# A gated state-space layer and a squared-ReLU FFN on one core: the order of all engines inside a batch, the FFN square, and TensorE's loop

## The reference

```python
def attn(x, A, B_w, B_b, C_w, C_b, D_w, D_b, s_w1, s_b1, s_w2, s_b2, g_w, g_b):
    s = sigmoid(silu(x @ s_w1.T + s_b1) @ s_w2.T + s_b2)
    u = (x @ B_w.T + B_b) * s
    # h_t = h_(t-1) @ A.T + u_t, over the 1024 tokens of a batch; hs holds all h_t
    y = hs @ C_w.T + C_b + x @ D_w.T + D_b
    return y * sigmoid(x @ g_w.T + g_b)

def ffn(x):                       # plus routed experts, weighted with trunc(softmax)
    return square(relu(x @ Ws1)) @ Ws2

x = x + layernorm(attn(layernorm(x)))
x = x + layernorm(ffn(layernorm(x)))
```

## Time and profile before

| | us |
|---|---|
| median of 3 runs | 936.57 (935.44 to 937.42) |
| profiled execution | 932.95 |
| its span, first to last instruction | 931.2 |
| TensorE busy | 857.2 (92%), 4120 matmuls |
| VectorE busy | 571.1 (61%) |
| GpSimd busy | 435.1 (47%) |
| ScalarE busy | 306.7 (33%) |
| DMA | 72.91 MB, mean 78 GB/s |

### The profile page before, as it was taken

One profiled execution on the slowest core, in us unless ns is written; L12 is line 12 of the kernel. 1 busy time (PEld: TensorE's weight loads), 2 busy tenths in 40 slices (PEclk: granted clock), 3 DMA queues, 4 the chain that ended last, 5 costly groups with the idle time before them and its releaser, 6 DMA issues. The chain is left out here.

```text
span 931.2 us, 13126 instructions
## 1 busy us (share of the span) xinstructions
PE 857.2 (92%) x4120; PEld 700.5 (75%) x4120; DVE 571.1 (61%) x1344; ACT 306.7 (33%) x530; POOL 435.1 (47%) x537
## 2 busy tenths in 40 slices
PE   5589999999999999999999999999999999999974
PEld 3477877878777777877778787777777777787763
DVE  4826676477655775467753776557754677624653
ACT  3341333224332333323332233323333233422333
POOL 1342456264453545444462644535554444625455
PEclk9889999999999999999999999999999999999998
DMA  8221023122130222211222221302222120122112
GB/s 282 80 81 56 15 77 114 69 91 92 45 120 18 90 90 90 92 53 47 80 113 69 90 90 41 121 20 90 90 90 92 49 77 9 67 69 91 46 45 91
DMA packets 17289, 72.91 MB, mean 78 GB/s; under 512 B 2643, under 2 KB 5075, under 8 KB 11094
## 3 DMA queue, kind: packets, MB, share of 16 engines
q1 hardware_dynamic: 17238, 72.38, 22.0%
HBM read 38.82 MB, written 33.55 MB: 78 GB/s over the span
## 5 line engine op out<-in xcount | busy, mean ns | idle before, releaser
L1404 POOL TENSOR_TENSOR rsv<-rsv,negh 128x1 f32<-128x1 f32 x64 | 35.7, 559 | 159.1 <-DVE rsv L1083 159.1
L421 PE MATMUL TM<-gw_hi,xT_hi 128*128 128x512 f32 x256 | 107.7, 421 | 0.7 <-ACT apt L770 0.7
L421 PE MATMUL TM<-dw_hi,xT_hi 128*128 128x512 f32 x256 | 102.7, 401 | 0.8 <-ACT work L781 0.8
L423 PE MATMUL TM<-gw_hi,xT_lo 128*128 128x512 f32 x256 | 100.8, 394 | 0.0
L423 PE MATMUL TM<-dw_hi,xT_lo 128*128 128x512 f32 x256 | 100.5, 393 | 0.0
L422 PE MATMUL TM<-gw_lo,xT_hi 128*128 128x512 f32 x256 | 100.1, 391 | 0.0
L422 PE MATMUL TM<-dw_lo,xT_hi 128*128 128x512 f32 x256 | 99.7, 389 | 0.0
L842 ACT ACTIVATE work<-TM,nmz,rsz 128x512 f32<-128x512 f32 x62 | 48.2, 778 | 148.3 <-POOL nmz L1414 148.3
L1440 POOL TENSOR_TENSOR xres<-work,xres 128x512 f32<-128x512 f32 x64 | 83.7, 1308 | 6.0 <-DVE work L1087 5.9
L1079 DVE TENSOR_TENSOR work<-TM,work 128x512 f32<-128x512 f32 x64 | 44.0, 688 | 67.1 <-PE TM L423 67.1
L1444 POOL TENSOR_TENSOR work<-work,xres 128x512 f32<-128x512 f32 x62 | 81.8, 1324 | 6.3 <-ACT work L842 6.3
(11 more groups left out here) (145 smaller groups left out, 2110.5 us busy)
## 6 DMA issues: line engine op xcount, KB each, us to landing
xin<-in_x SPq DMA_DIRECT2D x16, 1024.0 KB, 6.2
xres<-in_x SPq DMA_DIRECT2D x16, 1024.0 KB, 5.5
x_scratch<-xres SPq DMA_DIRECT2D x16, 1024.0 KB, 4.8
out<-work SPq DMA_DIRECT2D x30, 512.0 KB, 2.7
xres<-in_g_w_t SPq DMA_DIRECT2D x1, 1024.0 KB, 6.8
xres<-in_D_w_t SPq DMA_DIRECT2D x1, 1024.0 KB, 7.6
work<-in_Ws SPq DMA_DIRECT2D x2, 512.0 KB, 8.8
out<-work SPq DMA_DIRECT2D x4, 256.0 KB, 2.0
```

The lines of the kernel that those rows point to most:

```text
L421: eng.matmul(ps, lhs[0], rhs[0], start=first, stop=False)
L423: return eng.matmul(ps, lhs[1], rhs[0], start=False, stop=last)
L1404: return eng.tensor_tensor(dst, src, negh[:, 0:n], ALU.pow)
```

## The change

It has five parts.

1. The order in which each engine's queue takes the helpers inside a batch is another one, for batches 0 to 6. `tail_and_scan` becomes `first_tail` (batch 0, as before), `tail` and `last_tail`; `body` is new, `last_body` is the old order without the `prep` parts. The orders of batch 7 are the old ones.
2. The FFN square: ScalarE's Square writes h2_hi directly instead of hf. VectorE's h2 multiplies max(bank, 0) with hf (the Relu) into a part of w_first and subtracts h2_hi from it, giving h2_lo. GpSimd's h2_low is gone, as is VectorE's copy.
3. The FM bank of W1f is free when VectorE has made its square (sq_ok), not after the Relu (relu_ok).
4. TensorE's loop over batches 1 to 6 is written out by Python's `range`; the other engines keep theirs.
5. Four waits of TensorE for a high part are left out, where the wait for the low part of the same tile follows.

The diff, cut to its core:

```diff
-        FM_FREED = {"w": "relu_ok", "h": "h1_ok", "b": "u_ok", "s": "s_ok"}
+        FM_FREED = {"w": "sq_ok", "h": "h1_ok", "b": "u_ok", "s": "s_ok"}
...
+        def h2_free(eng, i, rep, m):
+
+            if m:
+                eng.wait_ge(S["w2_done"], body_at("w2_done", i, m * MS - 1))
+            elif rep > 0:
+                eng.wait_ge(S["w2_done"], body_at("w2_done", i - 1, L - 1))
...
-                eng.wait_ge(S["hs_hi_ok"], body_at("hs_hi_ok", b, j))
                 eng.wait_ge(S["hs_lo_ok"], body_at("hs_lo_ok", b, j))
...
-                G(*a, 0, {2: 0})
-                W1f(*a, 1, 0, {0: 1, 2: 2})
-                W1f(*a, 1, 1, {0: 3, 2: 4})
-                G(*a, 1, {0: 5, 2: 6})
-                G(*a, 2, {0: 7, 2: 8})
-                W2(*a, 4)
-                scan_step(*a, 9)
-                W2(*a, 5)
-                scan_step(*a, 10)
-                G(*a, 3, {1: 11})
-                W2(*a, 6)
-                W2(*a, 7)
+                G(*a, 0)
+                scan_step(*a, 0)
+                W1f(*a, 1, 0, {0: 1, 2: 2})
+                scan_step(*a, 3)
+                W1f(*a, 1, 1, {2: 4})
+                scan_step(*a, 5)
+                G(*a, 1, {1: 6, 2: 7})
+                G(*a, 2, {1: 8})
+                scan_step(*a, 9)
+                W2(*a, 4)
+                W2(*a, 5)
+                G(*a, 3, {1: 10})
+                W2(*a, 6)
+                W2(*a, 7)
+                scan_step(*a, 11)
...
-            with eng.Fori(1, NB - 1) as b:
-                tail_and_scan(b, 1)
+            for b in range(1, NB - 1):
+                tail(b, 1)
                 body(b, 1)
...
                 eng.wait_ge(S["relu_ok"], body_at("relu_ok", i, KF * m + f))
-                eng.activation(hf_row(name), hf_row(name), ACT.Square).then_inc(S["sq_ok"], 1)
+                h2_free(eng, i, rep, m)
+                eng.activation(h2_hi[:, f, :], hf_row(name), ACT.Square).then_inc(S["h2hi_ok"], 1)
...
+                eng.wait_ge(S["relu_ok"], body_at("relu_ok", i, KF * m + f))
+                h2_free(eng, i, rep, m)
+                square = w_first[:, D:2 * D]
...
+                eng.scalar_tensor_tensor(out=square, in0=fm_bank(name)[:, :], scalar=0.0, in1=hf_row(name),
+                                         op0=ALU.max, op1=ALU.mult).then_inc(S["sq_ok"], 1)
                 eng.wait_ge(S["sq_ok"], body_at("sq_ok", i, KF * m + f))
-                eng.tensor_copy(h2_hi[:, f, :], hf_row(name)).then_inc(S["h2hi_ok"], 1)
+                eng.wait_ge(S["h2hi_ok"], body_at("h2hi_ok", i, KF * m + f))
+                eng.tensor_tensor(h2_lo[:, f, :], square, h2_hi[:, f, :].bitcast(F32), ALU.subtract)\
+                   .then_inc(S["h2lo_ok"], 1)
```

More of the change, by code:

```diff
@@ L1214, in body @@
             def body(b, rep):
                 a = (b, rep)
-                prep = rep + 1 < NB
+                attn(*a, 0)
+                attn_norm(*a, 0)
+                attn(*a, 1)
+                attn_norm(*a, 1)
+                hs_low(*a, 2)
+                x1_stats(*a, 0)
+                x1_stats(*a, 1)
+                ft_low(*a, 0)
+                attn(*a, 2)
+                attn_norm(*a, 2)
+                ft_low(*a, 1)
+                hs_low(*a, 3)
+                t_low(*a, 0)
@@ new lines, in body @@
+                attn(*a, 3)
+                x1_stats(*a, 2)
+                ln1_norm(b + 1, 4)
+                hs_low(*a, 4)
+                t_low(*a, 1)
+                ft_low(*a, 2)
+                ln1_norm(b + 1, 5)
+                hs_low(*a, 5)
+                attn_norm(*a, 3)
+                attn(*a, 4)
+                ft_low(*a, 3)
+                x1_stats(*a, 3)
+                hs_low(*a, 6)
+                attn(*a, 5)
+                hs_low(*a, 7)
+                attn_norm(*a, 4)
@@ new lines, in body @@
+                h1(*a, 0, 0)
+                h1(*a, 0, 1)
+                t_low(*a, 2)
+                t_low(*a, 3)
+                x1_stats(*a, 4)
+                attn_norm(*a, 5)
+                u_of(*a, 0)
+                ln1_norm(b + 1, 6)
+                x1_stats(*a, 5)
+                ln1_norm(b + 1, 7)
+                attn(*a, 6)
+                ft_low(*a, 4)
+                ft_low(*a, 5)
+                attn_norm(*a, 6)
+                h2(*a, 0, 0)
+                h2(*a, 0, 1)
```

630 lines of the change are left out of this document (361 added, 269 removed).

## The result

The changed kernel took 909.5 us (median of 4 runs, 908.57 to 910.27) against 936.67 (935.44 to 937.42), a ratio of 0.973 [0.971, 0.975]: faster by 27.2 us, where 35.6 were forecast. Its profiled execution took 909.91.

The account below looks back on a forecast made before the run. TensorE's own work and its few waits were taken to bound each loop batch; 5.7 us a batch, 34 over six, plus 0.1 (batch 0) and 1.5 (last batch) make 35.6, giving 901 us; own range 897 to 907, with rivals to 912.

Parts of the forecast that it names:

- The five waits: TensorE's waits at W2(7), T(0), FT(5), T(4), SG(1) in each loop batch all go: 5.4 us a batch.
- The residual waits: New small TensorE waits at scan steps 1, 7, 9 and T(5), charged 0.1 each: 0.4 us lost a loop batch.
- Neighbours: Isolated fp32 groups on TensorE fall from 26 to 20 a loop batch, 0.08 each: 0.5 us gained.
- TensorE's loop written out: TensorE's jump back at each loop batch's head goes: 0.16 us gained a batch.
- The square: FFN square with VectorE subtracting: zero in the loop (to +0.5), earlier W2(0) and W2(4) in the last batch, 1.5 together.
- Batch 0: FT(0) first waits for ln1_norm(0), Y(0) 3.4 us later; offset by waits and groups saved: net 0.1 gained.
- The sum: Six loop batches 34 us, first batch 0.1, last batch 1.5: 35.6 us gained in all.
- A: VectorE becomes late at scan steps 7, 9 and T(5), 1.6 us a batch more than charged: 10, 911 us; chance 0.15.
- B: A GpSimd chain is late at SG(1), the old 1.07 us wait stays: 6 us, 907; chance 0.08.
- C: TensorE's straight-line code must be fetched, 57 more instruction pieces at 2.0 us exposed: slower, 1015 us; chance 0.04.

Follow-up runs that it names:

- The splitting run: Four FT transposes drawn apart on TensorE, against the changed kernel with VectorE's loop written out, batch 0's FT(0) later and hs_low(3) earlier: 905.21 us.

## Why the prediction was right, and where its sizes were off

The time of 909.5 us lies 8.5 above the forecast's 901, outside its own range of 897 to 907 and inside the one that reaches over the rivals to 912. Two of its signs failed: a loop batch took 104.45 us, not 103.1 +- 0.7, and TensorE's waits in it were up to 0.65, not under 0.2. The others came: the wait of 3.78 before FT(0), L1455's group gone, VectorE busy for 33.3 us more, and the wait at W2(7) of the last batch (1.24).

*The five waits* were right, one by one, and with them the sign and nearly the size of a loop batch: 103.1 forecast, 104.45 measured, and 103.03 once the two residues were taken away. The forecast had seen what bounds the loop (TensorE alone) and what the order could give.

*The residual waits* were the step that failed. The part on the waits charged 0.1 each at four places (scan steps 1, 7 and 9, and T(5)), 0.4 us a batch; 1.4 came (104.45 - 103.03), at one of the four, scan step 1, and at Y(3), which it did not name. Scan step 1 was too cheap because the sum priced TensorE's jump from a row and VectorE's not at all: in the order of before that jump stands in an idle stretch of VectorE, and its first addition, though counted, made nobody wait. The Trainium skill, Runtime: NRT & Kernel Launch, Instruction fetch mechanics, says that a taken branch to code outside a small window stalls. The forecast looked for that on TensorE, where the changed order shows no cost at all; behind VectorE's jump the traces show 0.63 (2.52 - 1.89) that the run with its loop written out takes away. By that rule the trace agrees on VectorE, and so does the count of q14's pieces, 23 for 38. Y(3) was the other: "everything else has 0.6 or more" holds for hs_low(3) only at the 0.29 of the earlier trace rows, though the earlier trace rows show a VectorE operation of 0.54 stretched to 1.52 beside GpSimd. The forecast used that row only as an upper bound for the square.

*Neighbours* was mis-sized: 0.5 us a batch was forecast from the 0.08 behind each isolated group. The rows had the answer: a group of eight is followed by the next matmul after 0.79 and two groups of four after 0.35 each, and 2 x (0.35 + 0.08) is 0.86, 0.79 + 0.08 is 0.87. What merging saves behind a group it loses inside. The splitting run prices it at 0.01 to 0.05 for a group. Of the 5.8 us between 108.84 and 103.03, the gap at TensorE's jump has 0.16 and the six groups about 0.1; the five waits with their restarts have the rest, 5.5, where 5.4 were counted.

*TensorE's loop written out*: 0.8 us were forecast over the batches, and the kernel without it takes 0.8 more in its trace (1.3 timed), but by luck. The gap at TensorE's jump is gone with the loop kept as well, together with the wait ahead of it, and the 0.8 lies in VectorE's jumps. No run shows that this part of the change is worth more than nothing.

*The square*: right in the loop (nothing). In the last batch the 0.69 taken for the subtraction was 1.64 and 1.68 for the two that fall beside GpSimd's x1 and 0.69 to 0.75 for the two that do not; the forecast had 1.52 as its upper end. VectorE's square itself took 0.69, not 0.75. But the run with the square moved shows that even the right duration would not have brought the 0.5 us at W2(0): the chain over x1(7) bounds that batch. The mistake was to count a wait's end as the batch's end without asking what ends next. W2(4) waits 2.3 for 3.1 and starts 0.8 earlier, near the 1.0 forecast; TensorE comes to it 98.7 us behind G(0), for 98.6 before. Of the 1.5 forecast 0.8 came, then. The spans hide it: behind W2(4) the profiled execution of before ran at the full clock and that of after at half of it, -0.8 in sum. Where the second execution of the changed kernel kept the full clock, the last batch takes 116.1, 0.8 less than before.

*Batch 0*: the wait of 3.8 us was right to 0.1. What failed is the clock behind it, a term that the sum did not have: TensorE at half its clock (the spacing is 0.43 for 0.23, the lower of its two levels, 1.2 GHz) for 3 us, some 1.4 us lost. Together 0.1 gained was forecast, and 1.5 were lost (3.0 in the second trace, where it lasted 6 us). The trace of before had it to read, behind W2(0) of its last batch.

*The sum*: 7.7 us too much in the loop (34 - 26.3), 1.6 in batch 0, 2.3 in the last batch, and 0.9 in the stretch before the first scan, which the change does not touch (65.9 to 67.4 over the runs). That is 12.5, as by the spans (35.6 - 23.1). The timed gain is 27.2 and not 23.1 because the profiled execution of before stood 3.7 below its median and that of after 0.4 above; a third of what the terms overshot was given back by that, which is luck. What lies behind the 3.7 can be seen: of 46 runs of the kernel before on the three chips, those under 934 us had a mean granted clock of 0.986 or 0.987 and those above 936.5 one of 0.981 to 0.985. The run with VectorE's loop written out in the order of before comes to W2(4) at the same time (101.7 us behind G(0)) and takes 17.7 us from there at half the clock, for 15.2.

*The rivals*: A (VectorE late) is what partly came, with other places than the three it named and 6 us more than charged, (1.4 - 0.4) x 6, instead of 10. B did not come: no wait at SG(1). C did not either. It had taken q14's 38 pieces for TensorE's; the pieces that grow with TensorE's program are q8's, 33 instead of 13. The 20 more cost nothing that the spacing of matmuls shows, and with the loops of four engines written out a loop batch stays at 103.03.

## What to carry to other kernels

When TensorE is the bound and waits in a few places, reordering is worth just those waits, and the new order has to be checked for what other engines' loops cost at the seam: a jump or a counted wait that was hidden beside an old stall is exposed when the stall goes. Price each VectorE operation that the new order puts beside a GpSimd addition at its stretched duration, small ones too, and move it away; here that, VectorE's loop written out and one misplaced transpose of batch 0 put right gave half as much again as the whole change. Before shortening a wait, ask whether what stands behind it is already late for another reason. And compare stretches only between cuts that have the same work in them, and only at the same clock.
